# Source rows picked by one-hot products on TensorE instead of gathers, in one group of seven

## What is computed

```
x, y = h[src], h[dst]                       # rows of the node table, one per edge
msg = einsum('eb,ebo->eo', w_comp[etype], einsum('ei,bio->ebo', x, weight))
a = tanh(relu(sum((x @ A1.T + b1) * (y @ A2.T + b2 + rel_emb[etype]), -1) / sqrt(32)))
nei = segment_sum(a[:, None] * msg, dst)
h_new = relu(nei + h[src[last edge of each dst]] @ self_loop_weight)
```

## Time and profile before

| | |
|---|---|
| median of 3 runs | 1353.69 us |
| the profiled execution's own time | 1355.84 us |
| its span in the trace | 1354.0 us |
| busy: PE, DVE, POOL, ACT | 943.7, 926.2, 756.1, 636.1 us |
| granted TensorE clock, mean of the span | 0.635 of full speed |

### The profile page before, as it was taken

How to read it: one execution, slowest core, us unless ns; L and a number is a source line. 1 busy time by engine, 2 the same in 40 slices (tenths; PEclk the granted TensorE clock), 3 DMA queues, 4 the chain that set the end, 5 groups by cost and what they waited for, 6 DMA issues and landing times.

```text
span 1354.0 us, 53620 instructions
## 1 busy us (share of the span) xinstructions
PE 943.7 (70%) x21540; PEld 843.1 (62%) x21540; DVE 926.2 (68%) x3188; ACT 636.1 (47%) x1731; POOL 756.1 (56%) x793
## 2 busy tenths in 40 slices
PE   3268777666666666666666666666664696999997
PEld 3257666555555555555555555555554696899997
DVE  8279988666776667667666666666754798555556
ACT  1147766545555555455455545455559783000000
POOL 5777777777777777777777777777750000000000
PEclk9556756555555555555555555555556898999999
DMA  4622111111111111111111111111100000000000
GB/s 99 80 56 55 41 41 40 46 45 39 38 36 33 39 40 40 40 39 40 39 40 39 39 39 40 39 40 39 18 12 14 2 4 2 4 4 4 5 4 17
DMA packets 58572, 44.98 MB, mean 33 GB/s; under 512 B 41920, under 2 KB 54560, under 8 KB 58320
## 3 DMA queue, kind: packets, MB, share of 16 engines
q1 hardware_dynamic: 33296, 28.65, 7.6%
q0 software_dynamic: 25024, 12.86, 6.4%
HBM read 38.37 MB, written 3.07 MB: 31 GB/s over the span
## 4 chain that ended last, share of the span: by engine, by line
POOL 41%; issue 21%; PE 16%; DVE 13%; DMA 6%; SPq 2%; ACT 1%; DVEq 0%; POOLq 0%; ACTq 0%
POOL arena L541 41%; PE ps L757 12%; DMA arena<-line_table 2%; DMA arena<-x_pad,arena 2%; DVE arena L1199 2%; DVE arena L1364 1%; DVE arena L1384 1%; PE ps L680 1%; DVE arena L1197 1%; PE ps L728 1%; DMA agg_table<-arena 1%; SPq L442 1%; DMA dst_parts<-arena 1%; DVE arena L1227 1%; PE ps L626 1%
## 5 line engine op out<-in xcount | busy, mean ns | idle before, releaser
L541 POOL DMA_INDIRECT arena<-x_pad,arena x782 | 754.3, 965 | 238.6 <-issue 236.2
L661 PE MATMUL ps<-arena 128*128 128x175 bf16 (+3 forms) x1567 | 199.1, 297 | 199.6 <-DVE arena L1199 199.1
L680 PE MATMUL ps<-arena 128*32 128x44 f32 (+3 forms) x7832 | 239.8, 262 | 96.2 <-DVE arena L1227 96.1
L661 PEld LDWEIGHTS ps<-arena 128*128 128x128 bf16 x1567 | 146.7, 131 | 217.5 <-DVE arena L1199 216.3
L680 PEld LDWEIGHTS ps<-arena 128*32 128x32 f32 x7832 | 182.1, 156 | 142.9 <-DVE arena L1227 122.5
L1199 DVE TENSOR_SCALAR arena<-pair_no,arena 128x275 bf16<-128x275 f16 (+2 forms) x784 | 237.3, 307 | 0.0
L952 ACT ACTIVATE arena<-arena 128x4 f32<-128x4 f32 x196 | 40.3, 206 | 384.7 <-DVE arena L1213 382.1
L1212 DVE TENSOR_TENSOR arena<-ps,arena 128x132 f32<-128x132 f32 x196 | 57.5, 294 | 238.2 <-DMA arena<-x_pad,arena 235.1
L757 PE MATMUL ps<-arena,adj_words 128*128 128x64 f16 (+1 forms) x6250 | 195.3, 193 | 24.2 <-DVEq L1314 20.9
L757 PEld LDWEIGHTS ps<-arena,adj_words 128*128 128x128 fp8e4 x6250 | 193.1, 98 | 26.2 <-DVEq L1314 21.6
L1227 DVE TENSOR_TENSOR arena<-ps,arena 128x768 f32<-128x768 f32 x196 | 187.9, 959 | 6.7
(11 more groups left out here) (196 smaller groups left out, 1095.0 us busy)
## 6 DMA issues: line engine op xcount, KB each, us to landing
arena<-line_table SPq DMA_DIRECT2D x28, 602.0 KB
arena<-x_pad,arena POOLq DMA_INDIRECT x782, 3.3
arena<-line_table SPq DMA_DIRECT2D x28, 140.0 KB
arena<-dst_parts SPq DMA_DIRECT2D x196, 5.7 KB
agg_table<-arena SPq DMA_DIRECT2D x196, 2.5 KB
dst_parts<-arena SPq DMA_DIRECT2D x1, 918.8 KB, 12.5
feat_table<-rows SPq DMA_DIRECT2D x1, 800.0 KB, 14.5
x<-x_pad SPq DMA_DIRECT2D x1, 400.0 KB
```

What stands on the lines that cost most here:

```text
L541: pool.indirect_dma_start(to, None, table, bass.IndirectOffsetOnAxis(ap=index, axis=0)).then_inc(done, 16)
L661: mm = nc.tensor.matmul(ps[:, at + d0 * BLOCKS:at + d1 * BLOCKS], row_hot[:, h, k, :], pair_hot[:, h, k, (d0 - first) * BLOCKS:(d1 - first ...
L680: return nc.tensor.matmul(to.rearrange("p (d m) -> p d m", m=MIX_COLS)[:, :, 0:m1 - m0], rows_of_slot, factors[:, :, m0:m1], start=False, ...
```

## The change

In every line but the last, one group (its number is 10, 17, 24, ... 192: 27 groups) no longer gets its source rows from gathers. They are picked out of an on-chip copy of the features by one-hot products:

- Prologue: SP loads the source numbers of the 27 groups (`pick_rows`, 27 x 512). DVE turns each source s into a code, 128 * (s / 512) + s mod 128, which is stored to memory (`pick_table`); it makes a mask of which of four blocks of 128 nodes a source lies in, and splits `x` into three bf16 parts (`x_parts`) that add up to it.
- SP, behind the two loads of a line: one load of 512 codes, repeated over 128 partitions (128 KB).
- DVE: in the line's second group four, in its third group three comparisons of 128 x 512 codes with a partition number (`make_pick_hots`); in the first group of the next line a product of PSUM with the mask and a sum over the four blocks, into `xp` (`read_picked`).
- PE: in each of the line's last four groups 21 matmuls of 128 x 128 by 128 columns (`pick_tile`, one slot of the picked group), between `count` and `sum_mixed`. They write to PSUM bank 7.
- POOL: no gathers for the 27 groups, 108 of the 782.
- The numbers 0 to 11 and 1 to 12 move from PSUM bank 7 to SBUF, since that bank is taken. `aggT` takes 128 partitions instead of 33; the picks use it as room for `pick_hot` and `x_parts`. POOL makes one more small table (`pick_no`).

```diff
+PICK_AT, PICKS = LINE + 3, LINES - 1
+PICKED = range(PICK_AT, PICK_AT + PICKS * LINE, LINE)
+PICK_WIDE = 4
+PICK_DEEP = -(-BLOCKS // PICK_WIDE)
+HOTS_AT = ((1, range(0, 4)), (2, range(4, PICK_DEEP)))
...
@@ SP, prologue
             sp.dma_start(line_table.rearrange("j (p e) -> p j e", p=LINE_ROWS), line_parts).then_inc(lines_stored, 16)
+            sp.dma_start(pick_line, pick_rows).then_inc(pick_loaded, 16)
+            sp.wait_ge(codes_made, 1)
+            sp.dma_start(pick_table, pick_codes).then_inc(codes_stored, 16)
             sp.wait_ge(parts_split, 1)
@@ SP, sweep, behind the two loads of line c
+                        if c < PICKS:
+                            if c >= 2:
+                                sp.wait_ge(pick_hots, c - 1)
+                            sp.dma_start(codes[:, c % 2, :], pick_table[c:c + 1, :].to_broadcast([P, WINDOW]))\
+                              .then_inc(code_in[c % 2], 16)
@@ POOL
                 for g in range(AHEAD, GROUPS):
-                    pool.wait_ge(mixed_used, g - AHEAD + 1)
-                    gather_group(g)
+                    if g not in PICKED:
+                        pool.wait_ge(mixed_used, g - AHEAD + 1)
+                        gather_group(g)
@@ PE
+                def pick_tile(c, k):
+                    if k == 0:
+                        pe.wait_ge(pick_hots, c + 1)
+                        pe.wait_ge(pick_read, c)
+                    at = PICK_AT_BANK + k * PICK_WIDE * FEAT
+                    for j in range(PICK_DEEP):
+                        for t in range(3):
+                            mm = nc.tensor.matmul(ps[:, at:at + PICK_WIDE * FEAT], pick_hot[:, j, k * P:(k + 1) * P],
+                                                  x_parts[:, t, j * PICK_WIDE:(j + 1) * PICK_WIDE, :]
+                                                  .rearrange("p b f -> p (b f)"),
+                                                  start=(j == 0 and t == 0), stop=(j == PICK_DEEP - 1 and t == 2))
+                    mm.then_inc(pick_out, 1)
...
+                    if g // LINE < PICKS and g % LINE >= LINE - SLOTS:
+                        pick_tile(g // LINE, g % LINE - (LINE - SLOTS))
                     sum_mixed(g)
@@ DVE, prologue
+            link(v.tensor_scalar(next_no[:], hot_no[:], 1.0, None, ALU.add))
+            dve.wait_ge(pick_loaded, 16)
+            link(v.tensor_scalar(pick_high, pick_line, 9, 7, ALU.logical_shift_right, ALU.logical_shift_left))
+            link(v.tensor_scalar(pick_low, pick_line, P - 1, None, ALU.bitwise_and))
+            link(v.tensor_tensor(pick_codes, pick_high, pick_low, ALU.add))
+            dve.sem_inc(codes_made, 1)
...
+            for w in range(PICK_WIDE):
+                link(v.tensor_scalar(pick_mask[:, :, :, w], pick_of, float(w), None, ALU.is_equal))
+            dve.wait_ge(inputs_loaded, 16 * LOADS)
+            link(v.memset(x_parts[:, :, BLOCKS:PICK_DEEP * PICK_WIDE, :], 0.0))
+            split(link, x[:], work[:], [x_parts[:, t, 0:BLOCKS, :] for t in range(3)])
+
             dve.wait_ge(q_made, 1)
@@ DVE, sweep
-                link(v.tensor_copy(hot_no_ps, hot_no[:]))
-                link(v.tensor_scalar(next_no_ps, hot_no[:], 1.0, None, ALU.add))
...
-                                         hot_no_ps.unsqueeze(1).to_broadcast(n),
+                                         hot_no[:].unsqueeze(1).to_broadcast(n),
...
+                def make_pick_hots(c, group):
+                    at, blocks = HOTS_AT[group]
+                    if group == 0:
+                        dve.wait_ge(code_in[c % 2], 16 * (c // 2 + 1))
+                    for j in blocks:
+                        last = v.tensor_scalar(pick_hot[:, j, :], codes[:, c % 2, :], pick_no[:, j:j + 1], None, ALU.is_equal)
+                    if group == len(HOTS_AT) - 1:
+                        last.then_inc(pick_hots, 1)
+
+                def read_picked(c):
+                    dve.wait_ge(pick_out, SLOTS * (c + 1))
+                    n = [P, SLOTS * PICK_WIDE, FEAT]
+                    link(v.tensor_tensor(picked.rearrange("p (w f) -> p w f", f=FEAT),
+                                         ps[:, PICK_AT_BANK:PICK_AT_BANK + SLOTS * PICK_WIDE * FEAT]
+                                         .rearrange("p (w f) -> p w f", f=FEAT),
+                                         pick_mask[:, c].rearrange("p k w -> p (k w)").unsqueeze(2).to_broadcast(n), ALU.mult))
+                    dve.sem_inc(pick_read, 1)
+                    link(v.tensor_reduce(xp[:, PICKED[c] % AHEAD, :, 0:FEAT],
+                                         picked.rearrange("p (k w f) -> p k f w", k=SLOTS, w=PICK_WIDE), AX.X, ALU.add))
...
+                    for group, (at, _) in enumerate(HOTS_AT):
+                        if g % LINE == at and g // LINE < PICKS:
+                            make_pick_hots(g // LINE, group)
+                    if g % LINE == 0 and 1 <= g // LINE <= PICKS:
+                        read_picked(g // LINE - 1)
                     make_mixed(g)
```

More of the change, by code:

```diff
@@ L232, in gnn @@
         side = stay.cut(SIDES * 3 * REL_COLS, BF16, n=SIDE).rearrange("p (u j c) -> p u j c", u=SIDES, j=3)
+        codes = stay.cut(2 * WINDOW, F16).rearrange("p (h e) -> p h e", h=2)
+        pick_mask = stay.cut(PICKS * SLOTS * PICK_WIDE, F16).rearrange("p (c k w) -> p c k w", c=PICKS, k=SLOTS)
+        pick = Carver(aggT, NODES_PAD)
+        pick_hot = pick.cut(PICK_DEEP * WINDOW, BF16).rearrange("p (j e) -> p j e", j=PICK_DEEP)
+        x_parts = pick.cut(3 * PICK_DEEP * PICK_WIDE * FEAT, BF16).rearrange("p (t b f) -> p t b f", t=3, f=FEAT)
+        picked = work[:].rearrange("p b f -> p (b f)")[:, 0:SLOTS * PICK_WIDE * FEAT]
         prep = Carver(arena, ARENA)
@@ L249, in gnn @@
         norm_parts = prep.cut(2 * FEAT + 4, n=1)
+        pick_line, pick_high = rel_line[0:PICKS, 0:WINDOW], rel_line[0:PICKS, WINDOW:2 * WINDOW]
+        pick_low = dst_line[0:PICKS, 0:WINDOW]
+        pick_codes = dst_line[0:PICKS, WINDOW:2 * WINDOW].bitcast(F16)[:, 0:WINDOW]
+        pick_of = carried.bitcast(I32)[:, 0:PICKS * SLOTS].rearrange("p (c k) -> p c k", c=PICKS)
         sweep = Carver(arena, ARENA)
@@ L354, in gnn @@
         side_made = sem("side_made")
+        pick_loaded, codes_made, codes_stored = sem("pick_loaded"), sem("codes_made"), sem("codes_stored")
+        code_in = [sem(f"code_in_{h}") for h in range(2)]
+        pick_hots, pick_out, pick_read = sem("pick_hots"), sem("pick_out"), sem("pick_read")
         lines_ready, fetched = sem("lines_ready"), sem("fetched")
@@ L402, in gnn @@
         EDGE_LOADS = 5
-        CONSTANTS = 6
+        CONSTANTS = 7
         serial = {p: p * TILES for p in range(6)}
@@ L534, in _ @@
             numbers(side_no[:, 0:1], [[1, 1]], 0, 1)
+            numbers(pick_no[:], [[P, PICK_DEEP]], 0, 1)
             pool.memset(ident[:], 0.0).then_inc(constants_made, 1)
@@ L1208, in score_edges @@
                     dve.wait_ge(fetched, g + 1)
-                    tiles = min((g + 1) * SLOTS, TILES) - g * SLOTS
-                    earlier = sum(min((n + 1) * SLOTS, TILES) - n * SLOTS for n in range(g % AHEAD, g, AHEAD))
-                    dve.wait_ge(gathered[g % AHEAD], 16 * (earlier + tiles))
+                    if g not in PICKED:
+                        tiles = sum(min((n + 1) * SLOTS, TILES) - n * SLOTS for n in range(g % AHEAD, g + 1, AHEAD)
+                                    if n not in PICKED)
+                        dve.wait_ge(gathered[g % AHEAD], 16 * tiles)
                     link(v.tensor_tensor(product, fetched_of(g)[:, :, 0:SCORED], xp[:, g % AHEAD], ALU.mult))
@@ L1721 @@
         "x_pad": x_pad, "edges": edges,
-        "src_cols": columns(grouped[:, 0]), "dst_cols": columns(grouped[:, 1]), "next_cols": columns(after), "bases": bases,
+        "src_cols": columns(grouped[:, 0]), "pick_rows": grouped[:, 0].reshape(GROUPS, WINDOW)[PICK_AT::LINE][:PICKS], "dst_cols": columns(grouped[:, 1]), "next_cols": columns(after), "bases": bases,
         "dst_rows_in": grouped[:, 1].reshape(LINE_ROWS, -1), "rel_rows_in": grouped[:, 2].reshape(LINE_ROWS, -1),
```

16 lines of the change are left out of this document (10 added, 6 removed).

## The result

The changed kernel takes 1269.21 us (median of 4 runs, 1267.50 to 1271.07) against 1353.22 us for the kernel before in the same comparison: a ratio of 0.938, 95% interval 0.936 to 0.940. The forecast was 1275 us.

A forecast was written before the change was run, and what follows sets the result against it. Gathers on POOL bound the kernel, with SP's queue right behind; 22 lines at 30.9 us put line 27 at 868, plus 70 the last store at 938 instead of 1017.1, 79 us less: 1275 us, range 1254 to 1325.

The forecast's parts named there:

- POOL's 137 us: Gathers: dropping 108 of 782 saves 137 us if POOL stays the bound, giving 1217; a rival held unlikely.
- the forecast 866: Gathers on POOL: 674 at an unchanged 1.269 us each, so the last starts at 866 us instead of 1003.
- 0.33 + 0.5 on 30.0: SP's queue per line: codes' load adds 0.33 us issue and 0.5 us transfer to 30.0, making 30.8 us.
- the rival with the dear load: SP's queue: codes' load falls on the two busy DMA engines, 32.8 us a line or more, 1317 us; chance 0.10.
- Comparisons 1.8 us forecast: VectorE per line: seven comparisons of 512 columns at 0.26 us each, 1.8 us.
- 0.69 for the sum: VectorE in `read_picked`: the sum over 512 columns taken to cost the same as the product, 0.69 us.
- The prologue's added work: VectorE before the sweep: 7.2 us added, hidden in the 8.61 us idle before `q_whole`, so costing nothing.
- A tile in 2.3 and 1.3 us forecast: TensorE: 21 matmuls of 128 columns take 2.3 us at 0.50 of the clock, 1.3 us at full clock.
- The clock rose as reckoned: TensorE in a line's last four groups: 5 us at the slow rate, 0.9 groups, then full clock.
- The 29.8 us for the two halves: VectorE and TensorE per line: 16 us for four tile groups plus 13.6 for three others, just under SP's 30.8.
- The slower rival: Sweep lines: TensorE stays at 0.50 clock and a line's halves add to 35.6 us, 1397 us; chance 0.08.
- the rival with drift but without the faster clock: Sweep lines: halves drift but clock stays slow, about 33 us a line, 1340 us; 1320 to 1350 given 0.06.

The follow-up runs named there:

- the spread load in both kernels: Line's load over 86 partitions issued as two, over 80 and 6: in the changed kernel 1257.96 us, in the kernel before 1350.26 us.
- the spread version: Changed kernel with the line's load over 86 partitions issued as two, over 80 and 6: 1257.96 us, ratio 0.930 to the kernel before.
- the run with the numbers alone: Kernel before with only the numbers 0 to 11 and 1 to 12 moved from PSUM to SBUF: 1355.41 us, ratio 1.0030.
- the doubled tiles: Changed kernel with every matmul of the tiles done twice, 42 instead of 21 a tile: 1296.99 us, ratio 0.959 to the kernel before.

## Why the prediction was right

**What bounds it next.** The step that carried the forecast was to ask, before counting POOL's 137 us as a gain, who stands right behind it. SP's 30.0 us a line between 177 and 297 us gave the answer, and the spread load in both kernels showed it: nothing gained before, 11 us after. Without that step the forecast would have been 1217.

**POOL.** The count (674) was right, the pace was not: "At 1.269 us the last starts at 11.6 + 673 x 1.269 = 866 us" failed. It was 911.3, 1.337 us each, 45 us later. I had priced what the change adds on VectorE as VectorE's time alone. It also holds up the gathers: by 0.18 us a comparison in the kernel before, 0.21 in the spread version, 0.28 in the changed one. Over 189 comparisons these are 34, 40 and 53 us, so they cover most or all of the 45; the numbers in SBUF may have added some 4. It did no harm, and that was partly luck. The last gather has to start some 15 us before the last store ends even where gathers set the pace (1003.0 and 1017.4 before), so the forecast 866 left POOL about 53 us of room before 934, and the measured 911.3 left 8. The prediction weighed no term that could have used these up; with the spread load, and already without the codes' load, the gathers were part of the limit.

**SP.** Forecast 0.33 + 0.5 on 30.0, 30.8 us a line and 30.9 with some slack; measured 30.68, of which 0.4 to 0.6 are the codes' load. The rival with the dear load (32.8) is out.

**VectorE.** Comparisons 1.8 us forecast, 1.05 for four and 0.79 for three measured. The read was mis-sized: 0.69 for the sum, 1.025 measured (its 512 values are read with a stride, which may be why); 1.7 in place of 1.5 for product and sum. Moving the numbers to SBUF cost VectorE nothing, as taken (232 ns in place of 230 for the comparison of 48 columns in the run with the numbers alone). Busy 27.3 us a line, forecast 27 to 28. The prologue's added work, 7.2 us by forecast, lay in the gap of 8.61 and filled 7.4 of it.

**TensorE.** A tile in 2.3 and 1.3 us forecast, 2.34 and 1.27 measured. The clock rose as reckoned, if a little later: it was below full for 0.9 groups a line in the forecast and for 36 of 108 tiles, 1.3 a line, in the trace. The 29.8 us for the two halves with "the two can only drift a group apart" was too dear: in the spread version they took 28.1, at nearly the same clock, and the doubled tiles show TensorE with 4 us to spare where the prediction left it 1. The term was under SP's 30.8 either way and did not enter the sum. The slower rival would have needed 33.9 us a line; not even twice the matmuls bring it there.

**Sum.** Line 5 at 189.9 (forecast 187 or 188), line 27 at 864.8 (868), 69.2 us from there to the end of the last store (70): 934.0 against 938. The errors are 2, 5 and 1 us, the first late and the others early, so they partly cancel; the large one, on POOL, lay off the path. Two figures of the prediction are slightly wrong in themselves: the last store before ended at 1017.4 and not at 1017.1, and the rival with drift but without the faster clock, 33 us a line, gives about 1331 by the same terms and not 1340. Neither moves the forecast.

## What to carry to other kernels

Before counting the relief of a bound, look for a stretch of the same trace in which that bound had not yet caught up: who set the pace there is who will set it afterwards, with the change's own additions on top. A small DMA that the queue waits for, behind a large one that runs on two DMA engines, was held here for nearly all of the large one's time (13.5 us); a load over 86 partitions split into 80 and 6 brought that to 3.5 for one more issue. And where GpSimd's gathers run beside it, VectorE work of the kind compared here, 16-bit from SBUF to SBUF, should be charged twice: once as VectorE's time, once as the gathers' delay.

## What the hardware showed that I had not expected

- A comparison of 128 x 512 16-bit values in SBUF held back the gathers by 0.18 us in the kernel before, by 0.21 in the spread version and by 0.28 in the changed one, for 0.26 us of VectorE; one of 128 x 224 f32 values from PSUM by nothing that the last gather's start shows (1003.0 us with and without).
- A sum of 512 f32 values over a strided dimension took 1.025 us, 2.0 ns a value; a product of 512 out of PSUM 0.675.
- With the load on 80 and 6 partitions the DMA share was 0.77 and the rate 167 GB/s, against 0.24 and 70 GB/s with 86.
